# Two attention layers in a row: scores turned in two products instead of four, a ring for x, and new orders for every engine

## The reference, cut to what matters

```python
# layer 0, per batch
q = heads(x @ Wq.T);  k = heads(text @ Wk.T);  v = heads(text @ Wv.T)
out = softmax(q k^T / 4) @ v          # per head; 77 text tokens, no image tokens
x = out @ Wo.T + bo + x
# layer 1: 73 text tokens, 4 image tokens
probs_t = softmax(q k_t^T / 4);  text_out = probs_t @ v_t
qsem = l2norm(probs_t @ text);   sem = qsem @ l2norm(ip)^T
probs_ip = softmax(q k_ip^T / 4 + 0.5 * sem) * mask
out = text_out + probs_ip @ v_ip
x = out @ W_out + b_out + x
```

## Time and profile before

| | |
|---|---|
| time, median of 3 runs (lowest, highest) | 2448.13 us (2445.96, 2452.12) |
| span of the profiled execution, first to last instruction | 2447.7 us, 0.4 us below that median |
| PE, DVE, ACT, POOL busy, share of the span | 92%, 70%, 71%, 65% |
| mean granted TensorE clock | 0.981 |
| DMA queue of SP | 305.36 MB, 44.7% of 16 engines' time |
| chain that ended last | PE 46%, DVE 23%, ACT 7%, issue 5%, DMA 3% |

### The profile page before, as it was taken

One profiled execution on the slowest core, in us unless ns is written; L12 is line 12 of the kernel. 1 busy time (PEld: TensorE's weight loads), 2 busy tenths in 40 slices (PEclk: granted clock), 3 DMA queues, 4 the chain that ended last, 5 costly groups with the idle time before them and its releaser, 6 DMA issues.

```text
span 2447.7 us, 90636 instructions
## 1 busy us (share of the span) xinstructions
PE 2259.4 (92%) x35896; PEld 1464.0 (60%) x35896; DVE 1702.0 (70%) x2860; ACT 1728.4 (71%) x2604; POOL 1592.2 (65%) x1056
## 2 busy tenths in 40 slices
PE   8999958999999999999999999999999999999984
PEld 6777735655566665666556555666566655555642
DVE  5543425777777777777777777777777777777763
ACT  4332327778878777787787787877877787787861
POOL 4121135777777777777777776777777777777762
PEclk9999969999999999999999999999999999999996
DMA  9968622444444444444344444444444444444421
GB/s 275 281 209 235 194 89 70 117 115 117 118 114 114 118 115 116 118 115 117 111 118 119 115 114 114 113 118 115 115 118 118 114 113 115 114 119 116 119 80 56
DMA packets 338318, 310.92 MB, mean 127 GB/s; under 512 B 180224, under 2 KB 281856, under 8 KB 337920
## 3 DMA queue, kind: packets, MB, share of 16 engines
q1 hardware_dynamic: 337920, 305.36, 44.7%
HBM read 164.66 MB, written 105.98 MB: 111 GB/s over the span
## 4 chain that ended last, share of the span: by engine, by line
PE 46%; DVE 23%; ACT 7%; issue 5%; DMA 3%; SPq 2%; DVEq 0%; POOL 0%; ACTq 0%; POOLq 0%
PE psum L1065 12%; PE psum L966 10%; PE psum L1049 8%; PE psum L1028 7%; DVE q_low L1220 4%; ACT q_high L1136 4%; DVE mneg L1213 3%; PE psum L969 3%; ACT ef L1154 3%; DVE e L1235 3%; DVE sq L1254 2%; DVE outt L1313 2%; PE psum L1032 2%; PE psum L991 2%; DVE x1b L1313 1%
## 5 line engine op out<-in xcount | busy, mean ns | idle before, releaser
L1381 POOL TENSOR_TENSOR e<-ef,eh 73x1024 f32<-73x1024 f32 x320 | 681.1, 2129 | 300.4 <-ACT eh L1169 257.0
L1154 ACT ACTIVATE ef<-psum 73x1024 f32<-73x1024 f32 (+1 forms) x640 | 628.0, 1011 | 90.9 <-PE psum L1032 87.4
L1235 DVE TENSOR_TENSOR e<-psum,e 73x1024 f32<-73x1024 f32 x320 | 386.7, 1209 | 135.6 <-PE psum L1065 135.3
L1213 DVE TENSOR_REDUCE mneg<-psum 128x8 f16<-128x616 f32 (+3 forms) x512 | 446.9, 923 | 34.9 <-PE psum L991 34.1
L1065 PE MATMUL psum<-eh,gram 128*73 128x512 f16 x1280 | 340.9, 390 | 45.2 <-ACT ef L1154 16.0
L1049 PE MATMUL psum<-ef,values 128*32 128x256 f32 x5120 | 351.4, 389 | 7.7 <-DVE pip L1295 5.9
L1028 PE MATMUL psum<-q_high,keys 32*73 32x256 f16 (+2 forms) x6144 | 324.7, 258 | 34.0 <-DVE mneg L1213 21.6
L1169 ACT ACTIVATE eh<-ef 73x1024 f16<-73x1024 f32 x320 | 337.0, 1053 | 16.2 <-ACT ef L1154 0.4
L1220 DVE SCALAR_TENSOR_TENSOR q_low<-psum,q_high 128x640 f16<-128x640 f32 x128 | 105.5, 824 | 262.3 <-ACT q_high L1136 262.3
L1028 PEld LDWEIGHTS psum<-q_high,keys 32*73 32x73 f16 (+1 forms) x6144 | 186.9, 110 | 144.5 <-issue 68.7
L1162 ACT ACTIVATE ust<-psum 128x512 f32<-128x512 f32 x384 | 223.4, 594 | 67.1 <-PE psum L1049 60.5
(11 more groups left out here) (180 smaller groups left out, 4530.3 us busy)
## 6 DMA issues: line engine op xcount, KB each, us to landing
rb<-r_dram SPq DMA_DIRECT2D x128, 384.0 KB, 4.1
keys<-k_dram SPq DMA_DIRECT2D x128, 231.0 KB, 3.6
values<-v_dram SPq DMA_DIRECT2D x128, 192.5 KB
ust<-ust SPq DMA_DIRECT2D x512, 48.0 KB, 2.5
v_dram<-vst SPq DMA_DIRECT2D x64, 320.0 KB
out<-outt SPq DMA_DIRECT2D x64, 320.0 KB, 2.2
k_dram<-kst SPq DMA_DIRECT2D x32, 616.0 KB, 4.8
x<-in_x SPq DMA_DIRECT2D x32, 384.0 KB, 3.7
```

The lines of the kernel that those rows point to most:

```text
L1154: act.activation(ef[l][0:m, unit_heads(n), :].rearrange("t h s -> t (h s)"), src, ACT.Exp, scale=SM).then_inc(s_exp[l], 1)
L1213: dve.tensor_reduce(dst, o, AX_X, ALU.max, negate=True).then_inc(s_max[l], 1)
L1235: dve.tensor_tensor(rest, banks(l, f"u{k}", 2)[0:m, :, :], rest, ALU.mult).then_inc(s_wr, 1)
L1381: pool.tensor_tensor(e2[0:m, k, :, :], ef[1][0:m, unit_heads(k), :], eh[0:m, unit_heads(k), :], ALU.subtract).then_inc(s_e2, 1)
```

## The change

Turned scores: `turned_scores` makes two groups of products instead of four. For that, the heads' channels are interleaved (even and odd partitions belong to the two heads of a pair), and the operands are laid out by transfers. `ka` holds the high keys of one head in one half of the rows and its low keys in the other, `tq` the high queries of that head twice; one product then gives key high x query high and key low x query high. `ks` holds high keys on one half of the rows and ones (marks) on the other, and against them `tq` holds the low queries and the maxima. The new steps on SP are tq (`turn_queries`: two transfers of 320 KB for a layer and batch) and tm (`place_maxima`: two of 96 KB); PE's t now waits for tm alone. Keys are loaded in three transfers instead of one (231 KB in all, as before), sh becomes one transfer instead of four, rw one instead of two, rl two instead of one, and both layers share one `rb`. `r_dram` now has 4 rows of 3 KB for each of two transfers, where it had 16 rows for one. x lives in a ring of 6 tiles in which the residual, the layer's output and the result are made in place. The first part stores each key once instead of twice with zeros. All of `ORDER` and `USES` is new, banks of one use need no longer be neighbours, a use of two banks may start on the first while the second is still taken, and the first and last rounds follow orders of their own, `FIRST` and `LAST`.

```diff
 ORDER = {
     "pe": """
-        1u2/3 1a1/3 0t1/1 1q/2 0t2/1 0a0/1 1s0/2 0a1/1 1s1/2 0a2/1 1a2/3 1i/2 1u3/3 1m/2 1u4/3 1t0/2 0q/0
-        1n0/3 1n1/3 1p/4 0s0/0 1n2/3 1n3/3 1n4/3 0s1/0 1t1/2 1a0/2 1u0/2 1t2/2 1u1/2 1o/4 0m/0 0o/1 0t0/0""",
...
+        0m/1 1u0/3 0o/2 1u1/3 0t0/1 1a1/3 1u2/3 0t1/1 1q/2 0t2/1 0a0/1 0a1/1 1s0/2 0a2/1 1n0/3 1a2/3 1s1/2 0q/0 1u3/3
...
+FIRST = {
+    "pe": """
+        0q/0 0s0/0 0s1/0 0m/0 0t0/0 0t1/0 0a0/0 0t2/0 0a1/0 0a2/0 0q/1 0s0/1 0s1/1 0m/1 0t0/1 0o/0 0t1/1 0a0/1 1q/0
...
+LAST = {
+    "pe": """
+        1a0/2 0m/0 1t2/2 0o/1 1u0/2 1u1/2 0t0/0 1a1/2 1u2/2 0t1/0 1q/1 0t2/0 0a0/0 0a1/0 0a2/0 1s0/1 1n0/2 1a2/2 1s1/1
...
 USES = [
-    "0t3/1 0a0/1 0a2/1 1u3/3 0q/0 0s0/0 0s2/0 1u1/2 0m/0 0t1/0",
...
+    "1u1 1u2 0t4 1n 0s0 0s3 1t4",
...
+def in_order(engine):
+
+    cycle = [step_of(word) for word in ORDER[engine].split()]
+    begin = [step_of(word) for word in FIRST.get(engine, "").split()]
+    end = [(l, B - 1 - before, name, n) for l, before, name, n in map(step_of, LAST.get(engine, "").split())]
+    lags = max(lag for _, lag, _, _ in cycle)
+    middle = [(l, i - lag, name, n) for i in range(B + lags) for l, lag, name, n in cycle if 0 <= i - lag < B]
+    whole = begin + middle[len(begin):len(middle) - len(end)] + end
+    assert sorted(whole) == sorted(middle)
+    return whole

...
+def load_key_tiles(sp, ka, ks, src, loaded):
+
+    both_parts = src.rearrange("a x (r f) n -> (a r) x (f n)", f=2)
+    sp.dma_start(ka[:].rearrange("p f n -> p (f n)"), both_parts).then_inc(loaded, 16)
+    for e in (0, 1):
+        high = src[:, 0, 1 - e:P:2, :].rearrange("a r n -> (a r) n")
+        sp.dma_start(ks[1 - e:P:2, e, :, :], high.unsqueeze(1).to_broadcast([HALF, 2, KC])).then_inc(loaded, 16)
+
...
+        xr = [early.xin] + [sb(f"x_ring{n}", [P, CW, S]) for n in range(1, RING)]
...
+            def turn_queries(l, b, n):
+
+                b.reached(sp, f_t[l], CW, 0)
+                b.reached(sp, s_ql[l], 1, 1)
+                for e in (0, 1):
+                    rows = qq[l][1 - e:P:2, :, :].rearrange("p h n -> p (h n)")
+                    sp.dma_start(tq[l][:, e, 0:2 * QW], rows.unsqueeze(1).to_broadcast([HALF, 2, 2 * QW]))\
+                      .then_inc(s_tq[l], 16)
+
+            def place_maxima(l, b, n):
+
+                b.reached(sp, s_tq[l], 32, 32)
+                b.reached(sp, s_mt[l], 1, 1)
+                for e in (0, 1):
+                    dst = tq[l][e:P:2, e, QW:].rearrange("p (c s) -> p c s", c=CW)
+                    sp.dma_start(dst, mt[l][e:P:2, :].unsqueeze(1).to_broadcast([HALF, CW, S])).then_inc(s_tm[l], 16)
...
-                for j in range(NJ):
-                    sp.dma_start(ust[l][j * SLOT + D:(j + 1) * SLOT, b.parity(), 0, :, :],
-                                 ust[l][j * SLOT:j * SLOT + D, b.parity(), 1, :, :]).then_inc(s_num[l], 16)
+                sp.dma_start(ust[l][1:P:2, b.parity(), 0, :, :], ust[l][0:P:2, b.parity(), 1, :, :]).then_inc(s_num[l], 16)
...
-                for copy in (0, 1):
-                    dst = r_dram[l][b.parity()][:, copy, :].rearrange("h (q i) -> h q i", i=QS)
-                    sp.dma_start(dst, rd[l][:, b.parity(), :]).then_inc(s_rw[l], 16)
+                dst = r_dram[l][b.parity()].rearrange("j r (q i) -> (j r) q i", i=QS)
+                sp.dma_start(dst, rd[l][:, b.parity(), :]).then_inc(s_rw[l], 16)
 
             def spread_inverses(l, b, n):
                 b.reached(sp, s_at[l], 1, 0)
-                b.reached(sp, s_rw[l], 32, 32)
-                src = r_dram[l][b.parity()].rearrange("h k n -> (h k) n").unsqueeze(1).to_broadcast([2 * HC, D // 2, CW * S])
-                sp.dma_start(rb[l][:].rearrange("p c s -> p (c s)"), src).then_inc(s_rb[l], 16)
+                before = spread_before(l, b)
+                if before is not None:
+                    sp.wait_ge(s_at[before[0]], before[1] + 1)
+                b.reached(sp, s_rw[l], 16, 16)
+                for r in (0, 1):
+                    src = r_dram[l][b.parity()][:, r, :].unsqueeze(1).to_broadcast([NJ, D, CW * S])
+                    sp.dma_start(rb[r:P:2, :, :].rearrange("p c s -> p (c s)"), src).then_inc(s_rb[l], 16)
 
...
                         tiles = [(slice(j * SLOT, (j + 1) * SLOT), banks(l, "t4", 4)[0:n, j, e * TS:(e + 1) * TS])
                                  for j in range(NJ)]
-                        cols, many = slice(2 * S, PW), TS
-                    for low, q in ((0, qh[l]), (0, ql[l]), (1, qh[l])):
-                        for rows, o in tiles:
-                            pe.matmul(o, keys(l, low, c)[rows, e, 0:n], q[rows, cols], start=(low == 0 and q is qh[l]),
-                                      stop=False)
+                        cols = slice(2 * S, PW)
                     for rows, o in tiles:
-                        k, lead = (2 * c + e, 0) if c < 2 else (2 * c, e * many)
-                        mm = pe.matmul(o, sel[rows, k, 0:n], mt[l][rows, lead:lead + many], start=False, stop=True)
+                        pe.matmul(o, paired_keys(l, e, c)[rows, 0:n], tq[l][rows, e, cols], start=True, stop=False)
+                    for rows, o in tiles:
+                        mm = pe.matmul(o, marked_keys(l, e, c)[rows, 0:n], tq[l][rows, e, QW:2 * QW][:, cols], start=False,
+                                       stop=True)
                 mm.then_inc(f_t[l], 1)
 
...
-                b.reached(act, (s_x, s_xo[0])[l], (16, 1)[l], (16, 1)[l])
-                b.reached(act, s_xo[l], 1, -1)
+                b.reached(act, s_xl[l], 1, 1)
+                data = x_of(b)
                 for c in range(CW if l == 0 else 2):
-                    ins = act.activation(res[l][:, b.parity(), c * S:(c + 1) * S], xin[l][b.parity()][:, c, :], ACT.Identity,
-                                         bias=bias_sb[l][:, c:c + 1])
+                    ins = act.activation(data[:, c, :], data[:, c, :], ACT.Identity, bias=bias_sb[l][:, c:c + 1])
                 if l:
```

More of the change, by code:

```diff
@@ L142, with step_of @@
 }
 USES = [
[8 rows of a table removed]
-]
-def steps_of(engine):
-    out = []
-    for word in ORDER[engine].split():
-        step, lag = word.split("/")
-        name = step[1:].rstrip("0123456789")
-        n = step[1 + len(name):]
-        out.append((int(step[0]), int(lag), name, int(n or 0)))
-    return out
-LAGS = max(lag for engine in ORDER for _, lag, _, _ in steps_of(engine))
[8 rows of a table added]
+]
+def step_of(word):
+    step, number = word.split("/")
+    name = step[1:].rstrip("0123456789")
+    return int(step[0]), int(number), name, int(step[1 + len(name):] or 0)
@@ L176, in __init__ @@
     def __init__(self):
-        self.on, self.lag = [], {}
-        for words in USES:
-            self.on.append([])
-            for word in words.split():
-                use, lag = word.split("/")
-                self.on[-1].append(use)
-                self.lag[use] = int(lag)
-    def bank(self, l, use):
-        return min(r for r in range(BANKS) if f"{l}{use}" in self.on[r])
-    def wait(self, eng, sems, b, l, *uses):
+        self.on = [words.split() for words in USES]
+        self.earlier = {}
@@ new lines, in __init__, with filled @@
+        last = [None] * BANKS
+        for l, batch, name, n in in_order("pe"):
+            for use in self.filled(l, name, n):
+                for r in self.banks(l, use[1:]):
+                    self.earlier[use, batch, r], last[r] = last[r], (use, batch)
+    @staticmethod
+    def filled(l, name, n):
+        if name in ("s", "t"):
+            return [f"{l}{name}{k}" for k in (2 * n, 2 * n + 1) if name == "s" or k < UNITS]
+        if name == "n" and n:
+            return []
+        return [f"{l}{name}{n}" if name in ("a", "u") else f"{l}{name}"]
@@ L190, in wait, with banks @@
+    def banks(self, l, use):
+        return [r for r in range(BANKS) if f"{l}{use}" in self.on[r]]
+    def wait(self, eng, sems, b, l, *uses, only=None):
         wanted = {}
-        for use in (f"{l}{u}" for u in uses):
-            for line in self.on:
-                if use not in line:
+        for use in uses:
+            mine = self.banks(l, use)
+            for r in mine if only is None else mine[only:only + 1]:
+                if self.earlier[f"{l}{use}", b.index(), r] is None:
                     continue
-                k, back = line.index(use), 0
-                while True:
-                    k, back = (k - 1, back) if k else (len(line) - 1, back + 1)
-                    last = line[k]
-                    earlier = b.later(self.lag[use] - back - self.lag[last])
-                    if not b.fixed or 0 <= earlier.i + earlier.off < B or b.i + b.off + self.lag[use] - back < 0:
-                        break
-                if b.fixed and not 0 <= earlier.i + earlier.off < B:
-                    continue
+                last, batch = self.earlier[f"{l}{use}", b.index(), r]
@@ L204, in wait @@
                 kind = last[1:].rstrip("0123456789")
```

(16 more changed lines are left out.)

344 lines of the change are left out of this document (208 added, 136 removed), and 14 rows, old and new, of the table USES.

## The result

The changed kernel takes 2713.27 us (median of 4 runs, 2705.78 to 2715.96), the kernel before beside it 2449.61 us: 1.107 times as long (95% interval 1.1055 to 1.1093). The profiled execution spans 2703.9 us, at a mean granted clock of 0.943.

The account below looks back on a forecast made before the run. It took PE to bound the kernel before and a 30.8 us round through SP after: (30.8 - 31.84) x 64 = -67, ends -15, so 2447.7 - 82 = 2366 us, range 2288 to 2475.

Parts of the forecast that it names:

- PE sets the pace: Middle of the kernel before: PE busy 286.1 of 300 us, 4.6% idle, ACT 16% behind, so PE was the bound.
- The group's 0.113 us: Turned scores on PE: each group costs 0.113 us; leaving out half saves 2.25 us a round, 144 us in 64 rounds.
- I take a quarter of that difference: Spread of inverses to rb from 4 source rows: round through SP of 30 to 33.4 us, taken as 30.8.
- slow rival: Spread on four engines decides: SP round 33.4 us, 2475 to 2533 us; sign: rb above 8 us, `turned` waits over 3; 20%.
- The round through SP: SP's chain from one issue of nl to the next: about 30 us, with norms issued at 25.9 and landed at 29.4.
- Hidden, as volume: New tq and tm transfers: 1.70 MB, 6.4 us of all engines a round, beside 13.7 busy now; their volume is hidden.
- cover of 4.7 against 4.2 us: Before layer 0's t0: PE's u and o cover 4.7 us; copying, issuing and landing the maxima takes 4.2; just fits.
- SP has the room: SP's issues: sh and rw save about 3.2 us a round, tq, tm, keys and rl add about 5.6; SP can take it.
- The first part, "nothing": First part: half the key copies of ACT and DVE go, but PE is busy 55.9 of 60 us: no gain.
- In shorter pieces: nothing: Keys keep their 231 KB in shorter pieces, at no cost, since they are loaded a round ahead.
- The ends, -15: Own orders for the first and last rounds: a gain of 0 to 40 us, taken as 15.
- my sign for myself: Signs of the main forecast (49%): rb landing in 4 to 6 us, and PE idle before t0 for `turned`.

Follow-up runs that it names:

- Spread and turning at no price: Changed kernel, inverses spread from 16 source rows without extra stores, and query and maxima transfers only for the first batch: 2479.6 us, 1.012.
- one order throughout: Changed kernel without its own orders for the first and last rounds: 2731.4 us; with keys also stored in one run a partition, 2671.0 us.
- half products: Kernel before with half of the turned scores left out (only high x high products): 2430.4 us, ratio 0.991.
- free copies: Changed kernel, inverses spread from 16 source rows; three of four copies hold zeros from the first two batches on, without later stores: 2617.2 us, 1.069.
- wide_spread: Changed kernel with each inverse stored four times, so each spread transfer's source has 16 rows instead of 4: 2765.7 us, ratio 1.127.
- keys_in_one_run: Changed kernel whose first part stores the keys of 8 batches as one run a partition instead of 8 pieces: 2695.3 us, ratio 1.100.
- narrow_spread_before: Kernel before with the spread of the inverses in two transfers of 4 source rows each: 2694.8 us, ratio 1.096.
- wide_and_loads_by_act: Changed kernel with each inverse stored four times (16 source rows) and keys and values loaded by ScalarE's queue: 2928.1 us, ratio 1.197.

## Why the prediction was wrong, step by step

**The account.** Behind the first part the change cost 2379 - 2130 = 249 us. Spread and turning at no price give 258 back (119 and 135 each alone), one order throughout 12 to 24 (measured without the other two). What is left is then worth some 20 to 35 us, if these add up: halved scores, ring, new orders, of which the halving alone was 21 in the kernel before. The first part adds 14 in the runs of the result.

**"PE sets the pace"**: wrong. I took a busy share of 95% for a bound and gave each microsecond saved on PE its full worth. The half products showed 24 us for 144. The group's 0.113 us was right; after, the groups of t0 follow each other by 0.11 to 0.14 us:

```profile
1258.18 0.31 PE L1135 MATMUL psum<-turned,keys 32*73 32x256 f16 x4
1258.32 0.28 PE L1137 MATMUL psum<-turned,own_keys 32*73 32x256 f16 x4
1258.43 0.28 PE L1135 MATMUL psum<-turned,keys 32*73 32x256 f16 x4
1258.54 0.28 PE L1137 MATMUL psum<-turned,own_keys 32*73 32x256 f16 x4
```

**"I take a quarter of that difference", the spread**: the step that failed first. The full price that I had worked out was 5.4 us of landing, the quarter 1.35, and I put it on the round through the norms alone, with 0.8 us. I set the full price aside because the slow row was a read of short rows. Measured, the landing grew by 2.8 us in the median of each layer, the norms behind it were late by 2.2 us, and the whole was worth 119 us in the changed kernel, 1.8 us a round. The reason was not in any row. The Trainium skill ("DMA: Bandwidth & Descriptors", why a DMA increments its semaphore by 16) gives 16, 8 and 4 engines for 16, 8 and 4 rows of source. The traces agree, with 16, 9 and 5 updates a transfer, and so does the order of the times: nothing, 61 and 240 us. My slow rival was too dear in the landing and still too mild in the result (2475 to 2533): it followed one landing, where `ust` and `out` on the same queue were late too (6.3 against 2.5 us for `ust`, 6.7 against 2.2 for `out`; both 3.1 with free copies), and POOL's order passed the spread's lateness on to PE's q. A slow outcome had a chance of 20% in the prediction.

**The round through SP**: the right chain, mis-sized step by step. In the round shown, with my figures behind: `pip` stored to `pt` back 3.63 (3.0), to den 0.87 (0.6), den to `rd` stored 4.98 (2.7), to the spread 1.86 (3.0), to the norms stored 2.58 (2.3), their landing 5.63 (3.5), to the next `pip` 15.46 (14.35): 35.01 against 29.4. Den and norms make 4.4 of the 5.6 us. The norms are late by the spread ahead of them, for the most part: with 16 rows of source they land in 2.4 us, without the turning in 4.4. `den` is not, since it takes 4.1 us with 16 rows as well; I had priced it at the 2.17 of a `den` with little in front, and in the new order keys, queries and `pt` stand in front of it (ahead of queries and `pt` it takes 2.1).

**"Hidden, as volume", the turning**: about right for the bytes (19 us) and right for the cover of 4.7 against 4.2 us (PE's wait, 6 us), wrong in the sum, since "SP has the room". It issues for 25 of 35 us in order, and SP itself is a link of the round that decides. Eight more issues with their waits cost about 110 us; that they cost it by delaying the next link is my reading, since issues and waits were not tried apart.

**The first part, "nothing"**: wrong, 14 to 47 us. I read PE's share and not the queue's. "In shorter pieces: nothing" was meant for the loads; the stores got shorter pieces too, and stand in a part whose queue was busy 0.76 already.

**The ends, -15**: wrong in sign, +11 to +15.

**What was to show it**: rb landed in 6.6 and 7.4 us, between my sign for myself (4 to 6) and that for the slow rival (above 8, reached by a few); and PE did not wait for `turned` (9.4 us in 34 rounds), as I had put there too. From 1000 to 2200 us it waited 34.4 us for `xl`, 28.7 for the maxima, 25.5 for `al` and 21.8 for exponentials, to name the longest.

## What to carry to other kernels

Before a busy engine is called the bound, take half of its work away in an experiment and see whether the time follows; what PE lost in work here was worth a sixth in time, at 95% busy. A transfer is priced by its shape first: the outer step of its source, the length of its pieces, and what shares the queue with it; and each issue on an engine whose order closes a loop can count like work on the path. When a part of the program can move by itself, subtract its end before comparing two runs.

## What the runs showed of the hardware that I had not expected

With short pieces the same first part ended at different times in different groups of runs, by chip: at 334 us in the run of the result, for which no chip is on record, at 329 on a second chip, 328 and 329 (two kernels) on a third, 356 on a fourth, 355 to 358 (four kernels) on a fifth, 365 to 367 (three) on a sixth. With long pieces it ended at 318 us on three chips, the third and the sixth among them. The first part of the kernel before ended at 321.5 to 321.6 (three kernels) on the fourth, where the other took 356. No kernel with short pieces ran on two chips, so that the chip is the cause, and not something else of the group, is read from this and not shown. The loads of `kip` that mark the end, in wide_spread and in keys_in_one_run:

```profile
355.58 0.62 SPq L915 DMA_DIRECT2D kip<-kip_dram  x1
```

```profile
318.40 0.62 SPq L915 DMA_DIRECT2D kip<-kip_dram  x1
```

A PE with more idle time also ran at a lower granted clock: 1.00 with 286 and with 271 of 300 us busy, 0.98 with 262 in narrow_spread_before, 0.97 with 246 after, 0.91 with 251 in wide_spread, 0.88 with 241 in wide_and_loads_by_act (each 800 to 1100 us). Busy time alone doesn't order them, since 251 us went with a lower clock than 246. A mean under 1.00 is part of the stretch at 1.2 instead of 2.4 GHz. What it adds to the time of the slow kernels was not tried apart.
